# Splitting the second layer's weight loads, and filling 72 rows of each expert's page with the rest by two indirect transfers

## The chip, the cores and the metric

The kernel runs on one core of a Trainium2 chip. A core has TensorE (matmuls), VectorE, ScalarE, GpSimd and SyncE, each with its own instruction stream, and 16 DMA engines that all queues share. SyncE and ScalarE issue plain transfers on queues q1 and q10, GpSimd issues indirect ones on q0. The metric is the device time of one execution in microseconds, median over runs.

## The reference

Four blocks in a row over 64 x 32 tokens of width 256, each of the form `x = x + ffn(cond(x))`. The change touches the end of the first and the second, a mixture of 32 experts of which each token uses 4:

```python
x = x + L0_ffn(L0_cond(x, ...), W1, W2, W3)          # dense feed-forward, hidden width 1024
x = x + L1_ffn(L1_cond(x, ...), gate, gate_up_proj, down_proj)
...                                                   # L2: attention on a paged cache; L3: 8 experts, top 2

def L1_ffn(hidden_states, gate, gate_up_proj, down_proj):   # 32 experts, TOP_K = 4, INTER = 96
    x = hidden_states.reshape(-1, 256)
    routing_weights = softmax(x @ gate)
    top_k_weights, top_k_indices = top_k(routing_weights, 4)   # then normalised to sum 1
    g, u = split(einsum('TD,EDF->TEF', x, gate_up_proj), 2)
    next_states = einsum('TEF,EFD->TED', u * silu(g), down_proj)
    return (next_states * router_weights[..., None]).sum(axis=1)
```

## The kernel before, in words

**First layer (L0), to about 204 us.** Four chunks of 512 tokens (`NCH`), eight hidden pieces each (`M0`). For each piece TensorE makes gate and up (`pe_gate_up`, L447), ScalarE applies silu (L487), VectorE multiplies, and TensorE multiplies down. Between the pieces of chunk c the routing of chunk c-1 for the second layer (called L1 in the code) is done: `pe_rows` (L524), `act_logits` and `act_copies` (L555, L562: each token's row copied four times into `outrows`), VectorE's top-k and slots, `dve_share_half` (L608).

**Scatter into pages.** `sent_d` in DRAM has a region of `SPAN1` = 2176 rows for each of the 32 experts, a row being 260 words (1040 bytes): the token's 256 values, its pair number, its weight. GpSimd scatters each chunk's rows there (`pool_send`, L783, 16 indirect transfers of 128 rows per chunk). `outrows` is used again for each chunk, so `act_copies` of the next chunk waits on `sent` (tiles 0 and 1) or `sent_late` (tiles 2 and 3).

**Fills.** The experts are computed in blocks of 128 rows, so rows after an expert's last token up to the block's end must hold a harmless row (zeros, and a pair number `FAR` that a later bounds check drops). After the last chunk VectorE writes the end row of each expert (`dve_ends`, L653, semaphore `tables`) and then the table of blocks. SyncE (L908 to L910, even experts) and ScalarE (L1192 to L1194, odd ones) each read 16 end rows into a register and issue one fill each: 128 rows from that row on, out of the tile `filler`, of which each partition holds `FILL` = 8 filler rows, so 16 partitions of 8320 bytes (`fill_rows`, L788). One more fill, of the spare page, comes at L905.

**What SyncE's queue does in order, as far as it matters:** segment stores to `newblk` (L870, L872), wait for VectorE's `dest`, three small stores to `dest_d` (L877) and a read-back (L879), a load of `shift` (L881), `tok_d` stores, then gate weights (L890, 3 MB into `big`), wait for the scatters of chunk 1 (`sent_late`), up weights (L892, 3 MB), wait for the end of the first layer, down weights (L899), fills, key load (L914), wait for all 33 fills and all scatters (L916 to L918), then block loads (`sp_block`, L769).

**Expert blocks (L1), from about 262 us.** 95 blocks (`NBK`) in a pipeline: SyncE loads 128 rows, TensorE transposes (L689), makes gate and up (L699), transposes and multiplies down (L717); ScalarE copies and silu (L728, L733), VectorE L745 to L758, GpSimd scatters results to `back_d` (L774). TensorE starts when `big1` says that both weights have landed.

Of the kernel before, what the change touches and what calls it, by code (L numbers as in the profile page):

```python
# [7 lines left out]
ALU = mybir.AluOpType  # L8
# [17 lines left out]
E1, K1, F1 = 32, 4, 96  # L26
E3, K3, F3, FS = 8, 2, 176, 704
# [7 lines left out]
ROW = BLOCK * 2 * G * HD  # L35
# [5 lines left out]
FAR = float(2 ** 17)  # L41
# [24 lines left out]
AT_FILLS, AT_COLS, AT_TABLE = range(1, 4)  # L66
O_CREDIT = 16
FILL = 8
# [5 lines left out]
def constants():  # L74
# [12 lines left out]
    def rows(x):  # L87
# [18 lines left out]
        "ones": np.ones((P, P)),  # L106
    }
# [43 lines left out]
L3 = Experts(E3, K3, 1, F3, ((0, HF3), (HF3, F3)), N3, NB3, NT, NCH + 1, NBK, NBK + NT, AT_TABLE)  # L151
# [18 lines left out]
def build(nc, a):  # L170
    (late_at, _), (first_at, _), (cast_at, _) = constants()
    with ExitStack() as ctx:
# [11 lines left out]
        def at(name, host, word, shape, dt=F32):  # L184

            return nc.alloc_sbuf_tensor_at(name, [P] + shape, dt, offset=base[host] + 4 * word).ap()
# [158 lines left out]
        L1.total = at("total", "rt0", 736, [TPC])  # L345
        L1.onehot = at("onehot", "maskb", 128, [TPC, K1, E1], BF16)
# [324 lines left out]

        def dve_table(dve, L, bank):
            dve.wait_ge(s["table_ps"], 1 if L is L1 else 2)
            nc.vector.tensor_copy(L.table_i[0:2, :], ps[0:2, bank, 0:P]).then_inc(s["tables"], 1)
# [113 lines left out]
        def fill_rows(r, e):  # L788
            p0 = (e * (P // FILL)) % P
            return sent_d[bass.ds(r, P), :].rearrange("(q r) n -> q (r n)", r=FILL), filler[p0:p0 + P // FILL, :]  # L790

# [51 lines left out]
        def _(sp):  # L843
# [29 lines left out]

            sp.wait_ge(s["index"], AT_DESTST)
            for j in range(NEWB):
                src = dest[(j % 2) * B:(j % 2 + 1) * B, (j // 2) * BLOCK:(j // 2 + 1) * BLOCK]
                sp.dma_start(dest_d[:, j * BLOCK:(j + 1) * BLOCK], src).then_inc(s["destld"], 16)  # L877
# [10 lines left out]
            sp.wait_ge(s["segst"], 32)  # L888
            sp.wait_ge(s["index"], AT_TOKST)
            sp.dma_start(l1_gate, a["gate1"]).then_inc(s["big1"], 16)  # L890
            sp.wait_ge(s["sent_late"], 2 * HALF_SENT)
            sp.dma_start(l1_up, a["up1"]).then_inc(s["big1"], 16)  # L892
# [24 lines left out]
            for name in ("sent", "sent_late"):  # L917
                sp.wait_ge(s[name], NCH * HALF_SENT)  # L918
# [40 lines left out]
            sp.wait_ge(s["tables"], AT_TABLE + AT_FILLS)  # L959
# [5 lines left out]
            sp.wait_ge(s["tables"], 2 * AT_TABLE)  # L965
# [24 lines left out]
        def _(pool):  # L990
# [22 lines left out]
            for c in range(NCH):  # L1013
                for h in range(2):
                    tiles, n = slice(2 * h, 2 * h + 2), 2 * c + h + 1
                    if c >= 1:
                        pool.wait_ge(s["sent_late" if h else "sent"], c * HALF_SENT)
                    pool.wait_ge(s["poolhigh"], n)
                    nc.gpsimd.tensor_scalar(outrows[:, tiles, :, D:D + 1].bitcast(I32),
                                            C["pairno"].rearrange("p (t k) -> p t k", t=TPC)[:, tiles, :].unsqueeze(3),  # L1020
                                            float(c * CH * K1), None, ALU.add).then_inc(s["poolhigh"], 1)
                    pool.wait_ge(s["poolhigh"], n + 1)
                    pool.wait_ge(s["numbered"], c + 1 + (h if c == NCH - 1 else 0))
                    pool.wait_ge(s["share_sb"], n)
                    for t in (2 * h, 2 * h + 1):
                        pool.wait_ge(s["rows_sb"], c * TPC + t + 1)
                        pool_send(L1, c, t)

# [321 lines left out]
        def _(dve):  # L1350
# [263 lines left out]
            dve_table(dve, L1, 6)  # L1614
            dve.wait_ge(s["keys"], 16)
# [331 lines left out]
        def _(pe):  # L1947
# [101 lines left out]
            pe.wait_ge(s["big1"], 32)  # L2049
# [409 lines left out]
```

## Time and profile before

| | |
|---|---|
| runs (median of 3, lowest, highest) | 1109.44 us, 1107.39, 1115.31 |
| profiled execution | 1108.0 us, span 1106.2 us |
| TensorE busy | 888.9 us (80%) |
| VectorE, ScalarE, GpSimd busy | 51%, 32%, 32% |
| moved by DMA | 132.3 MB, 120 GB/s on average |

The span is the time from the first to the last instruction of the profiled execution; the time lies 1.8 us above it. Times in rows are microseconds from the span's start. A row of a timeline gives the start, the duration of the group, engine and line, and in brackets how long the engine had been idle and what released it. A row of the busy time by stretch gives the stretch, its length, the busy time of TensorE, TensorE's weight loads, VectorE, ScalarE and GpSimd (with the number of instructions), then TensorE's granted clock, the busy share of the DMA engines and GB/s. TensorE's busy share is an average; what counts for an edit is the stretch that it touches.

### The profile page before, as it was taken

The numbers are of one execution on the slowest core, as the hardware profiler recorded it, in microseconds if no ns is written. First come the engines' busy times: TensorE is split into PE (matmuls) and PEld (weight loads), VectorE is DVE, ScalarE is ACT, GpSimd is POOL, SyncE is SP. The second block draws the span as 40 slices with busy tenths as digits, with TensorE's granted clock in tenths as the row PEclk, the third lists the DMA queues.
The fourth block names the chain that finished last, engine by engine and source line by source line (L and its number), as shares of the span: only waits on it lengthen the run. The fifth ranks groups of instructions, "written<-read, shape, count | busy, mean of one in ns | idle before, by whom it ended". The sixth has DMA issues, their size and how long they took to land.

```text
span 1106.2 us, 17591 instructions
## 1 busy us (share of the span) xinstructions
PE 888.9 (80%) x5301; PEld 684.8 (62%) x5301; DVE 567.5 (51%) x1670; ACT 358.5 (32%) x999; POOL 357.1 (32%) x385
## 2 busy tenths in 40 slices
PE   2999998604889989698147968897986998999976
PEld 2778776403677766574145757787643676777765
DVE  5647885421556645167426757755252434444322
ACT  3434333221333332021135656750252322222210
POOL 7100643550545555123433434200045201444000
PEclk9999999955999999898658888995995998999998
DMA  9151207765634442582257878600142202332231
GB/s 347 15 187 42 78 31 261 227 167 137 186 116 139 123 129 77 185 262 79 79 125 164 176 159 174 165 18 1 38 161 78 94 5 67 104 95 62 75 95 57
DMA packets 68205, 132.26 MB, mean 120 GB/s; under 512 B 19652, under 2 KB 50013, under 8 KB 65123
## 3 DMA queue, kind: packets, MB, share of 16 engines
q1 hardware_dynamic: 47123, 75.81, 23.1%
q0 software_dynamic: 20480, 53.19, 17.8%
q10 hardware_dynamic: 512, 2.13, 0.8%
q8 instruction: 47, 0.77, 0.3%
q14 instruction: 43, 0.35, 0.1%
HBM read 87.39 MB, written 43.30 MB: 118 GB/s over the span
## 4 chain that ended last, share of the span: by engine, by line
PE 30%; DMA 9%; issue 4%; DVE 3%; ACT 2%; SPq 1%; another core or an unknown queue 1%; POOL 1%; DVEq 0%; POOLq 0%; ACTq 0%
PE ps L447 8%; PE ps L699 4%; PE ps L717 3%; DMA early<-early 2%; DMA early<-newblk,new_i 2%; DMA big<-early 2%; DMA early<-in_cache,win_i 2%; PE ps L2329 2%; PE ps L2284 1%; PE ps L2181 1%; PE ps L2223 1%; SPq L945 1%; PE ps L2150 1%; DMA early<-big 1%; PE ps L2285 1%
## 5 line engine op out<-in xcount | busy, mean ns | idle before, releaser
L783 POOL DMA_INDIRECT sent_d<-mid,slot_i x88 | 98.5, 1119 | 122.4 <-DVE mid L608 74.3
L774 POOL DMA_INDIRECT back_d<-early,mid x95 | 93.7, 986 | 107.9 <-DVE early L758 74.2
L717 PE MATMUL ps<-early 96*128 (+1 forms) x346 | 99.3, 388 | 0.1
L745 DVE TENSOR_TENSOR early<-early,ps 128x96 f32<-128x96 f32 (+1 forms) x134 | 37.3, 278 | 119.0 <-ACT early L733 74.7
L728 ACT ACTIVATE early<-ps 128x256 f32<-128x256 f32 x134 | 51.3, 384 | 137.3 <-PE ps L689 130.0
L699 PE MATMUL ps<-big,early 128*128 x380 | 88.3, 356 | 5.8 <-ACT early L728 2.0
L481 DVE TENSOR_TENSOR hidl<-work,hidh 128x512 fp32r<-128x512 f32 (+1 forms) x56 | 38.8, 692 | 97.9 <-ACT hidh L474 96.5
L487 ACT ACTIVATE work<-ps 128x512 f32<-128x512 f32 (+1 forms) x56 | 33.4, 596 | 144.4 <-PE ps L447 138.2
L689 PE MATMUL ps<-late,mid 128*128 128x128 f32 x268 | 52.9, 280 | 33.4 <-DMA mid<-sent_d 33.4
L774 POOL DMA_INDIRECT back_d<-big,mid x39 | 38.4, 984 | 116.9 <-DVE big L758 112.7
L699 PEld LDWEIGHTS ps<-big,early 128*128 128x128 f32 x380 | 61.4, 195 | 19.7 <-issue 16.8
L689 PEld LDWEIGHTS ps<-late,mid 128*128 128x128 f32 x268 | 38.4, 145 | 49.0 <-issue 34.1
L733 ACT ACTIVATE early<-ps 128x96 f32<-128x96 f32 (+1 forms) x134 | 36.2, 270 | 90.8 <-PE ps L699 79.0
L1768 DVE TENSOR_REDUCE early<-ps 128x2 f32<-128x352 f32 x64 | 33.4, 522 | 57.5 <-PE ps L2150 54.6
L717 PEld LDWEIGHTS ps<-early 96*128 96x128 f32 (+1 forms) x346 | 55.4, 191 | 8.8 <-issue 3.5
L447 PE MATMUL ps<-yhigh,l_high 128*128 128x512 f32 x128 | 54.9, 429 | 4.6 <-DVE ylow L1524 3.1
L699 PE MATMUL ps<-early 128*128 x156 | 55.1, 478 | 3.6 <-ACT early L728 3.6
L2150 PE MATMUL ps<-early 128*128 128x176 f32 x256 | 56.8, 351 | 0.0
L1242 ACT ACTIVATE early<-ps,early 128x176 f32<-128x176 f32 x128 | 50.9, 406 | 10.9 <-DVE early L1772 9.7
L474 ACT ACTIVATE hidh<-work 128x512 fp32r<-128x512 f32 (+1 forms) x56 | 35.2, 628 | 52.9 <-DVE work L1545 37.5
L447 PE MATMUL ps<-ylow,l_high 128*128 128x512 f32 x128 | 51.3, 400 | 0.0
L447 PE MATMUL ps<-yhigh,l_low 128*128 128x512 f32 x128 | 51.2, 400 | 0.0
(388 smaller groups left out, 2098.3 us busy)
## 6 DMA issues: line engine op xcount, KB each, us to landing
mid<-sent_d SPq DMA_DIRECT2D x134, 130.0 KB
big<-back_d SPq DMA_DIRECT2D x16, 512.0 KB
early<-back_d SPq DMA_DIRECT2D x16, 256.0 KB, 3.4
early<-in_w SPq DMA_DIRECT2D x3, 1024.0 KB, 12.3
big<-in_gate SPq DMA_DIRECT2D x1, 3072.0 KB, 12.4
big<-in_up SPq DMA_DIRECT2D x1, 3072.0 KB, 11.0
early<-in_gu SPq DMA_DIRECT2D x1, 2816.0 KB, 10.5
big<-big SPq DMA_DIRECT2D x24, 96.0 KB
```

The source lines that it names most:

```text
L447: last = nc.tensor.matmul(out, w, x, start=start and n == 0, stop=stop and n == 2)
L481: nc.vector.tensor_tensor(low[0:w, slot, :], silu[0:w, slot, :], high[slot][0:w, :], ALU.subtract).then_inc(s["hid_ready"], 1)
L689: last = nc.tensor.transpose(ps[:, b % 2, k * P:(k + 1) * P], xblk[b % XRING][:, k * P:(k + 1) * P], ident)
L699: last = nc.tensor.matmul(ps[:, 2 + j % 2, 0:2 * F].rearrange("p (g n) -> p g n", g=2), L.yTb[j % 2][:, k * P:(k + 1) * P], L.gu[:, :, k, ...
L717: last = nc.tensor.matmul(ps[:, 6 + j % 2, 0:D], L.hTb[j % 2][0:f1 - f0, h * P:(h + 1) * P], L.down[0:f1 - f0, h, bass.ds(owners[j] * D, D ...
L728: nc.scalar.activation(L.yTb[b % 2], ps[:, b % 2, 0:2 * P], ACT.Copy).then_inc(s["turn_sb"], 1)
L733: nc.scalar.activation(L.sgb[(b - 1) % 2], ps[:, 2 + (b - 1) % 2, 0:L.F], ACT.Silu)\
L745: nc.vector.tensor_tensor(L.hb[j % 2], L.sgb[j % 2], ps[:, 2 + j % 2, F:2 * F], ALU.mult)\
L774: nc.gpsimd.indirect_dma_start(out=back_d, out_offset=bass.IndirectOffsetOnAxis(ap=xblk[b % XRING][:, D:D + 1].bitcast(I32), axis=0), in_= ...
L783: nc.gpsimd.indirect_dma_start(out=sent_d, out_offset=bass.IndirectOffsetOnAxis(ap=L.slot_i[:, i:i + 1], axis=0), in_=L.rows[c][:, t, n, : ...
L1242: last = nc.scalar.activation(Pex[:, n % 2, h, :], ps[:, 2 + n % 2, h * WK:(h + 1) * WK], ACT.Exp, bias=acol[:, 1, n % 2, h:h + 1], scale= ...
L2150: last = nc.tensor.matmul(ps[:, 2 + n % 2, h * WK:(h + 1) * WK], Qbd[:, (n // 2) % 2, n % 2, h * P:(h + 1) * P], KTs[:, n % 2, :], start=F ...
```

## The change

Three things change together.

1. The gate and up weights of the second layer are loaded in five pieces instead of two, each piece as soon as the part of `big` under it is free: of 6144 words per partition each, 4096 of gate after the segment stores, 3072 of up before the `dest_d` stores, and the other three pieces after the wait for `sent_late`. TensorE waits for 80 instead of 32.
2. A fill writes 72 rows instead of 128, as 18 partitions of 4 rows (4160 bytes each).
3. The rows from there to the block's end are written in aligned pieces of 8 rows. VectorE computes, for each of 32 x 8 possible pieces, its index, or one out of bounds where the piece lies behind the block's end (`dve_rest`). GpSimd writes them by two indirect transfers of up to 128 pieces of 8320 bytes each, after all fills have landed; SyncE waits for them on `sent`.

```diff
-FILL = 8
+FILL, FILLED, RUN = 8, 72, 4
...
+        def dve_rest(dve, ch):
+
+            piece, invalid, page_end = (L1.tabf[:, 0:E1], L1.ends[:, 0, :], L1.ends[:, 2, :])
+            ch.link(nc.vector.tensor_scalar(piece, L1.running, 1.0 / FILL, FILLED / FILL - 0.5 + 0.5 / FILL, ALU.mult,
+                                            ALU.add))
+            ch.link(nc.vector.tensor_scalar(piece, piece, MAGIC, None, ALU.add))
+            ch.link(nc.vector.tensor_scalar(piece, piece, MAGIC, None, ALU.subtract))
+            ch.link(nc.vector.scalar_tensor_tensor(page_end, L1.ends[:, 1, :], float(P), C["region"][:, 0:E1], ALU.mult,
+                                                   ALU.add))
+            ch.link(nc.vector.tensor_scalar(piece, piece, C["piece"], None, ALU.add))
+            ch.link(nc.vector.scalar_tensor_tensor(invalid, piece, float(FILL), page_end, ALU.mult, ALU.is_ge))
+            ch.link(nc.vector.scalar_tensor_tensor(piece, invalid, FAR, piece, ALU.mult, ALU.add))
...
+            ch.link(nc.vector.tensor_reduce(rest_f, by16, X, ALU.add))
+            nc.vector.tensor_copy(rest_i, rest_f).then_inc(s["tables"], 1)
...
         def fill_rows(r, e):
-            p0 = (e * (P // FILL)) % P
-            return sent_d[bass.ds(r, P), :].rearrange("(q r) n -> q (r n)", r=FILL), filler[p0:p0 + P // FILL, :]
+            n = FILLED // RUN
+            p0 = n * (e % (P // n))
+            return (sent_d[bass.ds(r, FILLED), :].rearrange("(q r) n -> q (r n)", r=RUN),
+                    filler[p0:p0 + n, 0:RUN * ROWW])
...
+            gate, up = a["gate1"].rearrange("p k n -> p (k n)"), a["up1"].rearrange("p k n -> p (k n)")
+            G1, U0, U1 = ROW, ROW + 4496 - KD * N1, ROW + 7568 - KD * N1
+            sp.wait_ge(s["segst"], 32)
+            sp.dma_start(big[:, 0:G1], gate[:, 0:G1]).then_inc(s["big1"], 16)
             sp.wait_ge(s["index"], AT_DESTST)
+            sp.dma_start(big[:, KD * N1 + U0:KD * N1 + U1], up[:, U0:U1]).then_inc(s["big1"], 16)
             for j in range(NEWB):
...
-            sp.wait_ge(s["segst"], 32)
             sp.wait_ge(s["index"], AT_TOKST)
-            sp.dma_start(l1_gate, a["gate1"]).then_inc(s["big1"], 16)
             sp.wait_ge(s["sent_late"], 2 * HALF_SENT)
-            sp.dma_start(l1_up, a["up1"]).then_inc(s["big1"], 16)
+            sp.dma_start(big[:, G1:KD * N1], gate[:, G1:KD * N1]).then_inc(s["big1"], 16)
+            for u0, u1 in ((0, U0), (U1, KD * N1)):
+                sp.dma_start(big[:, KD * N1 + u0:KD * N1 + u1], up[:, u0:u1]).then_inc(s["big1"], 16)
...
-            for name in ("sent", "sent_late"):
-                sp.wait_ge(s[name], NCH * HALF_SENT)
+            sp.wait_ge(s["sent_late"], NCH * HALF_SENT)
+            sp.wait_ge(s["sent"], NCH * HALF_SENT + 16 * E1 * FILL // P)
...
+            pool.wait_ge(s["tables"], AT_REST)
+            pool.wait_ge(s["filled"], 16 * (E1 + 1))
+            for j in range(E1 * FILL // P):
+                nc.gpsimd.indirect_dma_start(
+                    out=sent_d.rearrange("(q r) n -> q (r n)", r=FILL),
+                    out_offset=bass.IndirectOffsetOnAxis(ap=rest_i[:, j:j + 1], axis=0), in_=filler, in_offset=None,
+                    bounds_check=(SPARE1 + P) // FILL - 1, oob_is_err=False).then_inc(s["sent"], 16)
...
             dve_table(dve, L1, 6)
+            dve_rest(dve, ch)
...
-            pe.wait_ge(s["big1"], 32)
+            pe.wait_ge(s["big1"], 80)
```

Left out are two constants (17 columns of `late`), two small tiles, and the counts that `tables` has to reach in the second expert layer (L3 in the code), whose own fills (L961 to L964, 128 rows from 128 partitions) stay as they are.

## Rows read from the trace of the kernel before

**Rows 1.** Waits (us in total, times, longest), 200-265 us, TensorE and SyncE.
```profile
PE ps L689 <- DMA mid<-sent_d: 32.3, 1, 32.3
SPq L918 <- DMA sent_d<-work: 1.8, 1, 1.8
```

**Rows 2.** Busy time by stretch; last columns: TensorE's clock, DMA share, GB/s.
```profile
230.00:249.00 19.00, 0.59 (x2) 0.09 (x2) 1.88 (x11) 0.00 (x0) 12.70 (x14) 0.50 0.85 212
249.00:262.00 13.00, 0.00 (x0) 0.00 (x0) 0.00 (x0) 0.00 (x0) 0.00 (x0) 0.50 0.82 176
```

**Rows 3.** Timeline (start, duration, engine, line), SyncE and ScalarE, 229-287 us.
```profile
230.06 29.32 SPq L910 DMA_DIRECT2D sent_d<-work  x16
259.43 0.42 SPq L914 DMA_DIRECT2D zm<-in_first  x1
262.52 24.69 SPq L769 DMA_DIRECT2D mid<-sent_d  x17
229.72 27.25 ACTq L1194 DMA_DIRECT2D sent_d<-work  x16
```

**Rows 4.** Timeline, VectorE and GpSimd, 224 to 246 us.
```profile
224.84 0.17 DVE L608 TENSOR_TENSOR mid<-share,total 128x8 f32<-128x8 f32 x1
228.60 0.20 DVE L653 CAST endrow_i<-running 128x32 int32<-128x32 f32 x1
225.89 1.03 POOL L783 DMA_INDIRECT sent_d<-mid,slot_i  x1 [5.58 <-DVE mid L608]
245.43 0.96 POOL L783 DMA_INDIRECT sent_d<-mid,slot_i  x1 [0.30 <-issue]
```

**Rows 5.** Transfers (packets, MB, share of engines), GpSimd's queue, 248-249 us.
```profile
q0 software_dynamic: 14, 0.03, 7.7%
```

**Rows 6.** Timeline, ScalarE, two chunks of the first layer.
```profile
136.14 0.60 ACT L487 ACTIVATE work<-ps 128x512 f32<-128x512 f32 x1 [1.67 <-PE ps L447]
151.94 0.60 ACT L487 ACTIVATE work<-ps 128x512 f32<-128x512 f32 x1 [1.91 <-PE ps L447]
180.88 0.60 ACT L487 ACTIVATE work<-ps 128x512 f32<-128x512 f32 x1 [1.65 <-PE ps L447]
187.63 1.03 ACT L562 ACTIVATE mid<-ps 128x1024 f32<-128x1024 f32 x1 [3.73 <-DMA sent_d<-mid,slot_i]
198.88 0.60 ACT L487 ACTIVATE work<-ps 128x512 f32<-128x512 f32 x1 [1.47 <-PE ps L447]
```

**Rows 7.** Who waited for whom, 179 to 200 us, TensorE.
```profile
PE ps L536 <- DVE chosen L627: 2.2, 1, 2.2
```

**Rows 8.** Timeline, SyncE and GpSimd, 136 to 190 us.
```profile
136.92 1.73 SPq L877 DMA_DIRECT2D dest_d<-big  x3
165.85 0.34 SPq L881 DMA_DIRECT2D big<-in_first  x1
176.44 1.15 SPq L890 DMA_DIRECT2D big<-in_gate  x1
178.24 0.96 POOL L783 DMA_INDIRECT sent_d<-mid,slot_i  x1 [0.30 <-issue]
```

**Rows 9.** Busy time by stretch, first layer, 91 to 108 us.
```profile
91.00:108.00 17.00, 17.00 (x81) 13.71 (x80) 11.24 (x33) 8.85 (x14) 0.00 (x0) 1.00 0.01 1
```

**Rows 10.** Transfers by queue, 226-262 us: SyncE's (q1), ScalarE's (q10).
```profile
q1 hardware_dynamic: 656, 2.31, 35.7%
q10 hardware_dynamic: 512, 2.13, 24.0%
```

**Rows 11.** Timeline, SyncE, the later expert layer's fills.
```profile
867.29 8.42 SPq L964 DMA_DIRECT2D sent_d<-big  x8
```

**Rows 12.** DMA issues of the page (KB each, median us to landing).
```profile
big<-in_gate SPq DMA_DIRECT2D x1, 3072.0 KB, 12.4
big<-in_cache,seg_i POOLq DMA_INDIRECT x2, 8.5
```

**Rows 13.** Transfers, 797 to 815 us, where L954 and L958 run.
```profile
DMA packets 2275, 4.34 MB, mean 241 GB/s; under 512 B 354, under 2 KB 1762, under 8 KB 2274
```

More of the change, by code:

```diff
@@ L65 @@
 AT_CONDX, AT_TABST, AT_CONDIDX, AT_ROWPS, AT_DESTST, AT_SHIFT, AT_TOKST, AT_FOLDS = range(1, 9)
-AT_FILLS, AT_COLS, AT_TABLE = range(1, 4)
+AT_FILLS, AT_COLS, AT_TABLE, AT_REST = range(1, 5)
 O_CREDIT = 16
-FILL = 8
+FILL, FILLED, RUN = 8, 72, 4
 MAGIC = 1.5 * 2 ** 23
@@ L106, in constants @@
         "ones": np.ones((P, P)),
+        "piece": p[:, None] % FILL,
+        "pieceof": (p[:, None] // FILL) == np.arange(P // FILL)[None, :],
     }
@@ L150 @@
 L1 = Experts(E1, K1, 0, F1, ((0, F1),), N1, NBK, 0, 0, 0, 0, 0)
-L3 = Experts(E3, K3, 1, F3, ((0, HF3), (HF3, F3)), N3, NB3, NT, NCH + 1, NBK, NBK + NT, AT_TABLE)
+L3 = Experts(E3, K3, 1, F3, ((0, HF3), (HF3, F3)), N3, NB3, NT, NCH + 1, NBK, NBK + NT, AT_REST)
 L1.pieces = [(c, 0, TPC) for c in range(NCH - 1)] + [(NCH - 1, 0, 2), (NCH - 1, 2, TPC)]
@@ L345, in build @@
         L1.total = at("total", "rt0", 736, [TPC])
+        rest_f = at("rest_f", "rt0", 744, [E1 * FILL // P])
+        rest_i = at("rest_i", "rt0", 752, [E1 * FILL // P], I32)
         L1.onehot = at("onehot", "maskb", 128, [TPC, K1, E1], BF16)
@@ L670, in dve_ends @@
             nc.vector.tensor_scalar(cols2[:, 1:2], owner, float(E - 1), None, ALU.min).then_inc(s["tables"], 1)
+        def dve_rest(dve, ch):
[9 more added lines that the diff above has]
+            ch.link(nc.vector.scalar_tensor_tensor(piece, invalid, FAR, piece, ALU.mult, ALU.add))
+            by16 = piece.rearrange("p (j k) -> p j k", k=P // FILL)
+            ch.link(nc.vector.tensor_tensor(by16, by16,
+                                            C["pieceof"].unsqueeze(1).broadcast_to([P, E1 * FILL // P, P // FILL]),
+                                            ALU.mult))
+            ch.link(nc.vector.tensor_reduce(rest_f, by16, X, ALU.add))
+            nc.vector.tensor_copy(rest_i, rest_f).then_inc(s["tables"], 1)
         def dve_table(dve, L, bank):
@@ L958, in _ @@
                         sp.dma_start(L3.down[r0:r1, h, e * D:(e + 1) * D], a["down3"][p0:p0 + r1 - r0, m, :])                            .then_inc(s["down3"], 16)
-            sp.wait_ge(s["tables"], AT_TABLE + AT_FILLS)
+            sp.wait_ge(s["tables"], AT_REST + AT_FILLS)
             sp.wait_ge(s["fill_set"], 3)
@@ L964, in _ @@
                 sp.dma_start(sent_d[bass.ds(r, P), :], filler3).then_inc(s["filled"], 16)
-            sp.wait_ge(s["tables"], 2 * AT_TABLE)
+            sp.wait_ge(s["tables"], AT_REST + AT_TABLE)
             sp.wait_ge(s["filled"], 16 * (E1 + 1 + E3 + 1))
```

## The prediction

> **What bounds the kernel now.** I read the waits first, then the engines in the stretch that the longest wait names, then the transfers in it.
>
> The waits of TensorE between 200 and 265 us hold one that dwarfs the rest: 32.3 us in which its first transpose of the second layer's expert blocks (L689) waits for rows loaded from `sent_d` [rows 1]. The windows show what the core does meanwhile. From 230 to 249 us TensorE, VectorE and ScalarE are as good as idle while the DMA engines are busy 0.85 of the time at 212 GB/s; from 249 to 262 us no engine computes at all, and the DMA engines are busy 0.82 at 176 GB/s [rows 2]. So whatever shortens this stretch shortens the kernel, microsecond for microsecond, as long as its end is set by the same chain. What sets that end is the queues' work in order: VectorE gives the end rows of the 32 pages at 228.60, SyncE issues 16 fills from 230.06 for 29.32 us, ScalarE the other 16 from 229.72 for 27.25 us. SyncE then issues the key load at 259.43, waits 1.8 us for the last fill, and sends for the first block at 262.52 [rows 3, 4]. I put the landing of the last fill at 259.43 + 0.42 + 1.8 = 261.7. GpSimd's 16 scatters of the last token chunk run in the same stretch, issued from 225.89 to 246.4 [rows 4]. They are not last: from 248 to 249 us their queue moves 14 packets, 0.03 MB, its last of the stretch [rows 5]. The fills are last, by some 13 us.
>
> A second, small bound lies in the first layer. Its last token chunk goes slower than the one before. From the silu (L487) at 136.14 to the one at 151.94 four steps took 15.80 us; the same four from 180.88 to 198.88 took 18.00 us. Between them stands an idle time of 3.73 us in which ScalarE's copy (L562, at 187.63) waits for the scatters into `sent_d`, and TensorE waits 2.2 us for what follows from it [rows 6, 7]. The scatter it waits for was issued at 178.24, and the gate weights' 3 MB had been issued at 176.44 [rows 8]. A load of 3 MB and the scatters' packets shared the DMA engines, and the scatters came in 9 us after their issue. The last scatters of the next stretch took under 3.6 us (the last one issued at 245.43, landed by 249) [rows 4, 5].
>
> **The change, part by part.**
>
> *The weights.* 2.1 MB of gate go at the end of the segment stores (about 92 us), 1.6 MB of up ahead of the `dest_d` stores (136.92), and the rest, 2.6 MB, behind the wait for `sent_late`. At 91 to 108 us the DMA engines are busy 0.01 [rows 9]. What is moved past on SyncE's queue are the three small `dest_d` stores of 136.92, their read-back and the `shift` load; these would come about 5 us later, and between the stores at 136.92 and the issue of `shift` at 165.85 SyncE has only the read-back to do [rows 8]. So I cost it at nothing; the cover is over 20 us thick, and with it gone every late microsecond of the `dest_d` rows would hold VectorE's `token_rows`. What the weights give is not their own landing, since TensorE wants them only at 262. It is that no load is in flight beside the scatters that end with the one of 178.24. These then land by 178.24 + 3.6 = 181.8, before ScalarE asks (at 183.9, 3.73 us before its copy), and the wait goes. TensorE's chunk is then the one of 15.80 us: **-2.2 us**, which passes on to the residual, the routing and the fills. Bounds: 0, if another wait takes its place, and 3.7.
>
> *The fills.* Each fill shrinks from 128 rows of 1040 bytes to 72, so the 32 fills move 2.4 MB where they moved 4.26 MB (2.13 MB on each of the queues q1, with one spare page and the key load more, and q10) [rows 10]. Nothing in the number of issues changes. Two limits remain. The floor is the issue itself: one register load and one issue. The fills of the later expert layer (L964), eight in 8.42 us with the last taking 0.33, come every (8.42 - 0.33) / 7 = 1.16 us, and they are alone [rows 11]. The present pace is 29.32 / 16 = 1.83 us on average. The ceiling on pace while GpSimd scatters is the traffic. A scatter of 133 KB every 1.27 us (16 in 20.5 us) [rows 4] is 105 GB/s out of 212, which leaves 107 GB/s for a pair of fills, one from each queue. Such a pair is 150 KB now instead of 266, so 1.40 us instead of 2.5. Until the scatters are gone (by 249) that makes 13 pairs; the other three go at the floor. Last issue: 230.06 + 12 x 1.40 + 3 x 1.16 = 250.3; landed 1.5 later (as the 1.8 now, with less in it), 251.8. Against 261.7 that is **-9.9 us**. Bounds: all at the floor, last issue 247.5, landed 249.0, -12.7; and no gain at all, if something other than the bytes sets the pace (rivals).
>
> *The rest.* GpSimd now waits for all 33 fills and then issues two indirect transfers, for whose landing SyncE waits before the first block. This is new and lies wholly on the path. From VectorE's share (L608, ended 225.01) to GpSimd's first scatter at 225.89 it took 0.9; the second issue follows 1.3 after the first; the last scatter landed 2.6 to 3.6 after its start, of which I take 3.0 [rows 4, 5]. Sum: **+5.2 us**. The nearest row above it is the gather of 128 rows of 16 KB, 8.5 us to landing [rows 12], which would make 10.7. It moved 2.1 MB, though. Of the 2 x 128 pieces of 8.3 KB only those between row 72 after the end and the page's end are written; with ends spread evenly over a page, 56 of 128 experts need some and 28 rows on average, 12 rows per expert and about 0.4 MB in all, plus rounding. So I stay with the lower row. Bounds +4.8 and +10.7.
>
> *The ten VectorE operations* of `dve_rest` are about 0.2 us each and end before 236, while the fills run for another 15 us: nothing. What waits behind them on VectorE is the key load, which comes after the fills. Seventeen more columns of `late`: nothing. ScalarE issues its 16 fills as before. Behind GpSimd's new wait stand only the scatters of the blocks' results, which need the blocks first, so it delays nothing of its own.
>
> Sum on the profiled execution: 1108.0 - 2.2 - 9.9 + 5.2 = 1101.1. The median shown is 1.4 us above that execution, so the same sum on the median is **1102.5 us**, 0.6% less.
>
> **Rivals.**
>
> *Nine engines.* A fill used to be 16 rows of 8320 bytes, which 16 engines can share evenly. Now it is 18 rows of 4160 bytes. If a transfer only uses as many engines as divide its rows, that is nine with two rows each, 8320 bytes per engine, exactly what an engine carried before. The trace has a place to look: 26 loads of 8 to 88 rows together with one of 128 partitions leave 354 packets under 512 bytes [rows 13]. If each engine used leaves one completion packet, the 26 leave 338, which is 13 per load and not 16. The row counts follow from the code (88, 40, 48, 80, 8, ...), and the largest divisor up to 16 of each adds up to 338 exactly. So nine engines it very likely is. What I doubt is that this sets the pace: an engine's fills and scatters together are 4.26 + 2.13 MB over 16, 400 KB in 32 us or 12 GB/s, where the gate load's 3.1 MB in 12.4 us [rows 12] make 16 GB/s per engine, with scatters beside it. If it does set it all the same, the fills land at 261.7 as now and the new tail is simply added: 1109.4 - 2.2 + 5.2 = **1112.5**. This is the case on the other side. It decides as soon as the fills come in less than 3.0 us earlier than now.
> The Trainium skill, page "DMA: Bandwidth & Descriptors", section "Why a DMA increments its semaphore by 16 and not by 1", states the divisor rule itself: a transfer from SyncE or ScalarE is split over the largest number up to 16 that divides the slowest dimension of both sides. The 338 packets agree with it, and by it the fills run on nine engines.
>
> *The scatters, not the bytes, slow the issue.* Then the fills go on at one in (249 - 230) / 8 = 2.4 us, if half of them fall there, until the scatters are gone and at the floor after it: 8 done at 249, eight more at 1.16, landed at 259.8. Gain 1.9, tail 5.2, weights 2.2: +1.1, **1110.5**. For it: the pace. SyncE's 16 issues took 29.32 us [rows 3]; eight at 2.4 and eight at 1.3 make just that. Against: even without scatters 1.3 is above the floor of 1.16, with 176 GB/s moving [rows 2].
>
> *Everything at the floor.* Fills land at 249.0: -2.2 - 12.7 + 5.2 = -9.7, **1099.7**. For it: the steadier row of the later expert layer. Against: no scatters run beside that one.
>
> *The weights do nothing* and the wait at 187.63 has another source: 2.2 us more on each of the above.
>
> *A dear tail* of 10.7 adds 5.5 to any of them.
>
> **How the numbers follow.** The forecast has 0.50, nine engines 0.22, the scatters 0.10, the floor 0.13, and 0.05 for a dear tail or what I have not seen. The time is that of the likeliest, 1102.5, with its own range of 1099 to 1106. The whole range reaches from below the floor case to above nine engines: **1098 to 1114**. Within 1% (11.1 us, about what a measurement of this kernel can tell from no change) lie all the cases named at their own prices; over it on the fast side is only the floor with a stall less (0.12), on the slow side only nine engines with a dear tail (0.04).
>
> **What would show it.** Of the changed kernel: the copy at L562 of the last chunk no longer waits for `sent_d`, and four silu steps take 15.8. The 16 issues on each queue take about 20 us instead of 29 and 27. GpSimd's two transfers of fillers start about 252, and the first block's load about 5.5 us after. If the queues still take 27 us or more, the bytes were not the limit; if the first two transfers take over 8 us, the tail was mis-sized; if TensorE's wait for the first block is unchanged or longer, gain and tail have cancelled.

## The result, and the profile after

| | before | after |
|---|---|---|
| runs beside each other on one chip, median | 1110.08 us | 1115.94 us |
| lowest to highest | 1106.07 to 1115.31 | 1111.64 to 1121.46 |
| profiled span | 1106.2 us | 1114.1 us |

The changed kernel is slower: ratio 1.0066, 95% interval 1.0036 to 1.0096, so 4 to 11 us. That is still within 1%, but 13 us above the predicted time, beyond the upper end of the range, and of the other sign than the forecast.

The same stretch as in [rows 3, 4], start and duration of each group, SyncE, ScalarE and GpSimd of the changed kernel:

```profile
226.70 30.16 ACTq L1232 DMA_DIRECT2D sent_d<-work  x16
226.99 30.54 SPq L940 DMA_DIRECT2D sent_d<-work  x16
242.43 0.96 POOL L806 DMA_INDIRECT sent_d<-mid,slot_i  x1 [0.30 <-issue]
257.57 0.38 SPq L944 DMA_DIRECT2D zm<-in_first  x1
259.86 0.99 POOL L1062 DMA_INDIRECT sent_d<-work,rest_i  x1 [16.48 <-DMA sent_d<-work]
261.16 0.99 POOL L1062 DMA_INDIRECT sent_d<-work,rest_i  x1 [0.30 <-issue]
...
266.58 7.38 SPq L792 DMA_DIRECT2D mid<-sent_d  x7
```

The 16 fills take 30.54 us on SyncE where they took 29.32, although each moves little more than half the bytes. The busy time by stretch (as in [rows 2]: DMA share and GB/s last) says what did not hold them up:

```profile
230.00:249.00 19.00, 0.00 (x0) 0.00 (x0) 1.90 (x9) 0.00 (x0) 10.29 (x12) 0.50 0.47 145
249.00:258.00 9.00, 0.00 (x0) 0.00 (x0) 0.00 (x0) 0.00 (x0) 0.00 (x0) 0.50 0.38 103
```

The DMA engines fell from 0.85 and 0.82 busy to 0.47 and 0.38, and the issues did not speed up. And TensorE's wait for the first block, 32.3 us in [rows 1], grew (waits, 200 to 285 us):

```profile
PE ps L712 <- DMA mid<-sent_d: 39.6, 2, 39.3
POOL sent_d L1062 <- DMA sent_d<-work: 16.5, 1, 16.5
```

From the start: SyncE's first fill is issued 3.1 us earlier than before (226.99 against 230.06), the 16 issues cost 1.2 us more, and from the key load to the first block's load it takes 9.01 us instead of 3.09, so 5.9 more. 266.58 is 4.1 us later than 262.52. Another 3.8 us up to the end came behind this place; a second trace of the same kernel, below, doesn't have them.

### The profile page after: what moved, and what is told of

Its sections match the earlier page's. It is cut to its first block, busy times and chain, and to the rows that moved or that the text cites. A ratio compares the mean times of both kernels' runs of the same rounds, so it can differ in the third digit from the quotient of the medians.

```text
span 1114.1 us, 17609 instructions
## 1 busy us (share of the span) xinstructions
PE 886.1 (80%) x5301; PEld 682.8 (61%) x5301; DVE 570.3 (51%) x1680; ACT 357.9 (32%) x999; POOL 358.7 (32%) x387
## 4 chain that ended last, share of the span: by engine, by line
PE 27%; DMA 10%; issue 5%; DVE 3%; ACT 2%; SPq 1%; another core or an unknown queue 1%; POOL 1%; DVEq 0%; POOLq 0%; ACTq 0%
PE ps L451 8%; PE ps L722 4%; PE ps L740 3%; DMA big<-in_cache,win_i 2%; DMA big<-newblk,new_i 2%; DMA early<-in_cache,win_i 2%; PE ps L2368 2%; DMA early<-newblk,new_i 2%; PE ps L2220 1%; PE ps L2323 1%; PE ps L2262 1%; DMA early<-early 1%; DMA early<-big 1%; SPq L975 1%
## 5 line engine op out<-in xcount | busy, mean ns | idle before, releaser
L2189 PE MATMUL ps<-early 128*128 128x176 f32 x256 | 54.5, 340 | 0.0
L781 DVE TENSOR_SCALAR early<-ps,mid 128x256 f32<-128x256 f32 x95 | 45.1, 475 | 14.0 <-PE ps L740 11.9
L732 PE MATMUL ps<-late,early 128*96 128x128 f32 (+1 forms) x173 | 41.9, 279 | 11.7 <-DVE early L768 11.5
```

Source lines behind the costliest of these rows:

```text
L732: last = nc.tensor.transpose(ps[0:f1 - f0, 4 + j % 2, h * P:(h + 1) * P], L.hb[j % 2][:, f0:f1], ident)
L781: nc.vector.tensor_scalar(L.ob[j % ORING], ps[:, 6 + j % 2, 0:D], xblk[j % XRING][:, D + 1:D + 2], None, ALU.mult).then_inc(s["out_sb"], 1)
L2189: last = nc.tensor.matmul(ps[:, 2 + n % 2, h * WK:(h + 1) * WK], Qbd[:, (n // 2) % 2, n % 2, h * P:(h + 1) * P], KTs[:, n % 2, :], start=F ...
```

## The experiments

Three theories stood against each other after the trace above. **A:** while GpSimd issues its scatters, every instruction of SyncE's and ScalarE's sequencers is slow, and a fill is six of them (load of the end row into a register, two register operations, an assertion, a move, the issue), so neither bytes nor engines matter. **C:** nine engines set the pace. **D:** bytes or packets do after all. The view that separates them is how fast the queues issue while the scatters run (to about 245 us) and behind them.

**The weights alone** (`e1_weights`): the kernel before with these edits.

```diff
...
+            sp.wait_ge(s["segst"], 32)
+            sp.dma_start(big[:, 0:G1], gate[:, 0:G1]).then_inc(s["big1"], 16)
             sp.wait_ge(s["index"], AT_DESTST)
+            sp.dma_start(big[:, KD * N1 + U0:KD * N1 + U1], up[:, U0:U1]).then_inc(s["big1"], 16)
...
-            sp.dma_start(l1_gate, a["gate1"]).then_inc(s["big1"], 16)
             sp.wait_ge(s["sent_late"], 2 * HALF_SENT)
-            sp.dma_start(l1_up, a["up1"]).then_inc(s["big1"], 16)
+            sp.dma_start(big[:, G1:KD * N1], gate[:, G1:KD * N1]).then_inc(s["big1"], 16)
+            for u0, u1 in ((0, U0), (U1, KD * N1)): ...
```

> The kernel before with the weight loads alone split as in the changed kernel; fills of 128 rows, no rest. Theory A (the weights' part of the change is sound, the loss is all in fills and tail): the wait of the row copies for the scatters goes, four silu steps of the last chunk take 15.7 us instead of 18.0, the end rows come 1.7 to 3 us earlier, and the first block's load about 2 us before 262.5, total 1108 us (-2). Rival B (what the weights give is lost again in the expert blocks, since the changed kernel's blocks fell back by some 4 us between 262 and 453 us): the same first block load, but the blocks end no earlier than before, total 1110 us or more.

Measured: ratio 0.9985 (0.9956 to 1.0013), 1107.6 against 1109.4 us. The wait is gone, SyncE's first fill starts at 227.47 and the first block's load at 258.63. From VectorE's first result of a block to its last it took 171.8 us, where the two traces of before have 172.1 and 169.0, so nothing is lost in the blocks and B finds no support. (They end 4.9 us before those of the first trace of before, but only about half a us before those of the second.) The time agrees with A's 2 us, but can't tell it from nothing.

**Sixteen engines** (`e2_fills64`), the changed kernel with one number altered:

```diff
-FILL, FILLED, RUN = 8, 72, 4
+FILL, FILLED, RUN = 8, 64, 4
```

> The changed kernel with fills of 64 rows (16 partitions of 4160 bytes, so 16 engines of equal load) instead of 72 rows (18 partitions, nine engines); the rest starts one piece of 8 rows earlier. Theory A (while GpSimd scatters, each instruction of SyncE's and ScalarE's sequencers is slow, whatever the fill moves): SyncE's 16 issues still take 30 us (29 to 31.5), first block load at 266 to 267, total as the changed kernel, 1116 us. Rival C (nine engines set the pace): the packets spread over 16 engines, 16 issues in 20 us or less, first block load about 256, total 1106 us.

**A ninth of the rows** (`e3_fills8`): fills of 8 rows, now 8 partitions of one row (1040 bytes) each, and four indirect transfers for the rest:

```diff
-FILL, FILLED, RUN = 8, 72, 4
+FILL, FILLED, RUN = 8, 8, 4
...
-            n = FILLED // RUN
-            p0 = n * (e % (P // n))
-            return (sent_d[bass.ds(r, FILLED), :].rearrange("(q r) n -> q (r n)", r=RUN),
-                    filler[p0:p0 + n, 0:RUN * ROWW])
+            p0 = FILLED * (e % (P // FILLED))
+            return sent_d[bass.ds(r, FILLED), :], filler[p0:p0 + FILLED, 0:ROWW]
...
-            for j in range(E1 * FILL // P):
+            for j in range(2 * E1 * FILL // P):
                 nc.gpsimd.indirect_dma_start(
```

> The changed kernel with fills of only 8 rows (8.3 KB, a ninth of the bytes); four indirect transfers of up to 128 pieces write the rest. Theory A: the pace doesn't depend on the bytes; SyncE's 16 issues take 28 to 30 us while scatters run at 2.6 us a pair, and only the tail grows: four issues instead of two (+2.6 us) and about 2.1 MB instead of 0.6 (+5 to +8 us), first block load about 275, total 1124 us. Rival D (the bytes or the packets of the fills hold the issue after all, in queue or engines): the 16 issues take under 22 us, and the first block load comes at 266 or earlier, total 1115 us or less.

SyncE's timeline of the 64-row kernel, then of the 8-row one:

```profile
228.43 27.57 SPq L940 DMA_DIRECT2D sent_d<-work  x16
256.04 0.42 SPq L944 DMA_DIRECT2D zm<-in_first  x1
265.02 9.23 SPq L792 DMA_DIRECT2D mid<-sent_d  x8
```

```profile
227.95 29.83 SPq L940 DMA_DIRECT2D sent_d<-work  x16
257.82 0.38 SPq L944 DMA_DIRECT2D zm<-in_first  x1
271.26 3.70 SPq L794 DMA_DIRECT2D mid<-sent_d  x4
```

The 8-row kernel settles D. Its fills move 8 KB each, the DMA engines are nearly idle once the scatters are gone (stretches as above), and 16 issues still take 29.83 us:

```profile
230.00:245.00 15.00, 0.48 (x2) 0.00 (x0) 3.42 (x17) 0.00 (x0) 10.95 (x13) 0.50 0.31 108
247.00:258.00 11.00, 0.00 (x0) 0.00 (x0) 0.00 (x0) 0.00 (x0) 0.00 (x0) 0.50 0.06 12
```

Where the time is, the instructions of the two lines of a fill on SyncE show (count, then shortest, median and longest in ns, then first and last start). First while scatters run, 230 to 245 us:

```profile
L939 SPq TENSOR_LOAD <-endrow_i x5: 6/502/699, 229.5 to 243.0; - x5
L939 SPq SEQ_ASSERT  x5: 3/700/708, 230.9 to 243.8; - x5
L940 SPq FUSED_REGOPS  x5: 6/699/708, 230.9 to 244.5; - x5
L940 SPq DMA_DIRECT2D sent_d<-work x4: 13/696/709, 232.3 to 241.6; - x4
```

and behind them, 247 to 258 us:

```profile
L939 SPq TENSOR_LOAD <-endrow_i x8: 482/484/567, 247.4 to 256.5; - x8
L939 SPq SEQ_ASSERT  x8: 18/18/18, 248.1 to 257.3; - x8
L940 SPq DMA_DIRECT2D sent_d<-work x9: 316/316/317, 247.0 to 257.5; - x9
L940 SPq FUSED_REGOPS  x8: 37/37/37, 248.1 to 257.3; - x8
```

```profile
L939 SPq SEQ_ASSERT  x5: 7/11/207, 230.7 to 242.8; - x5
L940 SPq MOVE sent_d<-work x4: 3/479/700, 231.4 to 240.6; - x4
```

The start times of the records show the pattern. Beside the scatters SyncE gets on in steps of 0.70 us, with one to three instructions in a step, and a fill takes three to six steps. A fill costs (241.6 - 232.3) / 3 = 3.1 us in the 8-row kernel's first stretch and (257.5 - 247.0) / 8 = 1.31 in its second.

Full DMA engines alone don't do this. In the kernel before, behind the scatters, they are 0.82 busy at 176 GB/s ([rows 2]), and SyncE's small instructions are as quick there as anywhere, 249 to 262 us:

```profile
L909 SPq SEQ_ASSERT  x8: 18/18/18, 249.8 to 258.9; - x8
L910 SPq FUSED_REGOPS  x8: 37/37/37, 249.9 to 258.9; - x8
```

The 64-row kernel shows that C is not nothing either. SyncE's issues of line 940 after 245 us, changed kernel first, then 64 rows:

```profile
L940 SPq DMA_DIRECT2D sent_d<-work x10: 317/318/698, 244.9 to 257.2; - x10
```

```profile
L940 SPq DMA_DIRECT2D sent_d<-work x9: 314/314/315, 247.1 to 255.7; - x9
```

and ScalarE's, in the same order:

```profile
L1232 ACTq DMA_DIRECT2D sent_d<-work x7: 516/517/532, 247.4 to 256.3; - x7
```

```profile
L1232 ACTq DMA_DIRECT2D sent_d<-work x8: 2/322/322, 247.0 to 254.3; - x8
```

On sixteen engines a fill takes 1.08 us behind the scatters (8.6 / 8) and ScalarE's issue 322 ns; on nine it takes 1.37 (12.3 / 9) and 517. SyncE's own issue is no dearer, 318 ns against 314. What takes longer there is the load of the end row into a register, 247 to 264 us, changed kernel first, then 64 rows:

```profile
L939 SPq TENSOR_LOAD <-endrow_i x8: 489/536/804, 246.2 to 256.0; - x8
```

```profile
L939 SPq TENSOR_LOAD <-endrow_i x8: 266/270/274, 247.5 to 255.0; - x8
```

The 128-row fills of the kernel before, on sixteen engines, had 524 ns as the median of that load, and the 8-row fills 484, so the number of engines is not the only thing that lengthens it.

The packets of the changed kernel's fills are the count that nine engines leave: in 226 to 258.6 us ScalarE's queue moved

```profile
q10 hardware_dynamic: 432, 1.20, 13.1%
```

432 packets for 16 fills, 27 each: 18 of data and nine completions. The Trainium skill, page "DMA: Bandwidth & Descriptors", section "Why a DMA increments its semaphore by 16 and not by 1", gives the divisor rule, and the trace agrees.

The 27.57 us for 16 fills are neither A's 29 to 31.5 nor C's 20. Beside the scatters 64 rows are no faster than 128, but slower (the next section has a table); behind them the number of engines counts. The times: 64 rows 1.0003 (0.9970 to 1.0036), 1111.2 us, where A had 1116; 8 rows 1.0046 (1.0015 to 1.0077), 1116.4 us, where A had 1124. The first block's load came at 271.26 instead of the expected 275, since the bytes of four transfers took less time than I gave them.

**Fills behind the scatters** (`e5_late`): the 64-row kernel with two waits before the fills on both queues, and nothing else.

```diff
+            sp.wait_ge(s["sent"], NCH * HALF_SENT)
+            sp.wait_ge(s["sent_late"], NCH * HALF_SENT)
             for e in range(0, E1, 2):
```

> As the changed kernel with 64-row fills, but SyncE and ScalarE wait with their fills until all of GpSimd's scatters have landed (near 246 us). Theory A (only the scatters make the queues' instructions slow): the same 16 issues on each queue now come every 1.07 us from the first on, 16 to 17.5 us in all instead of 27.6; last issue near 263, first block load near 272, total 1118 us. Rival G (two queues at once, or the row registers, are slow by themselves): 22 us or more.

```profile
246.85 16.82 ACTq L1236 DMA_DIRECT2D sent_d<-work  x16
246.94 16.99 SPq L942 DMA_DIRECT2D sent_d<-work  x16
```

A gave 16 to 17.5 us; it is 16.99 instead of 27.57, with both queues working and the same registers. The fills started 18.5 us later and ended 7.9 us later, and the first block's load came at 273.01 (A: near 272). G falls. The time of the single run was 1113.98 us, 4 below what A said.

**Issues without registers** (`e6_static`):

```diff
             for e in range(0, E1, 2):
-                r = sp.value_load(L1.endrow_i[0:1, e:e + 1], min_val=e * SPAN1, max_val=e * SPAN1 + T)
-                sp.dma_start(*fill_rows(r, e)).then_inc(s["filled"], 16)
+                sp.dma_start(*fill_rows(e * SPAN1 + T, e)).then_inc(s["filled"], 16)
```

> All of the pages' fillers are written by six indirect transfers of GpSimd's; SyncE and ScalarE issue 16 fills each of 64 rows at the same time, but at fixed rows that nobody reads (row 2048 of each region), so without a register load: of the six instructions of a fill only the issue itself is left. Theory A (each sequencer instruction pays about 0.7 us while GpSimd issues indirect transfers, so the count of instructions sets the pace): 16 issues in 8 to 20 us, 0.5 to 1.3 us each, instead of 2.9 while scatters run. Rival H (the issue of a transfer alone is what is held up): the pace stays at 2.2 us or more while scatters run. The total says little; near 1110 us.

```profile
L948 SPq DMA_DIRECT2D sent_d<-work x16: 348/563/1256, 226.1 to 236.6; - x16
```

Sixteen issues in 10.5 us while scatters run, 0.70 each: with one instruction per fill instead of six the pace is about four times as high. H falls. The issue itself is slowed too, 563 ns instead of 314, but here the DMA engines are 0.87 busy at 237 GB/s, so the bytes may have a part in that. (This kernel's time, 1112.47 us in its single run, is no measure: its plain fills write rows that nobody reads.)

**Fewer plain fills** (`e4_hybrid`). If GpSimd goes on at its 1.27 us per transfer while the others crawl, it should have part of the fills. Experts 16 to 31 get no plain fill; VectorE computes for each the single rows up to the next multiple of 8 and the aligned pieces from there to the page's end. These touch nothing that another transfer writes, so GpSimd doesn't wait for `filled`:

```diff
+            ch.link(nc.vector.tensor_scalar(c8[:, G], L1.running[:, G], 1.0 / FILL, 0.5 - 0.5 / FILL, ALU.mult,
+                                            ALU.add))
...
-            for e in range(0, E1, 2):
+            for e in range(0, EH, 2):
...
-            pool.wait_ge(s["filled"], 16 * (E1 + 1))
+            pool.wait_ge(s["fill_set"], 2)
+            for j in range(2):
+                nc.gpsimd.indirect_dma_start(
+                    out=sent_d.rearrange("(q r) n -> q (r n)", r=FILL), ...
+            nc.gpsimd.indirect_dma_start(
+                out=sent_d, out_offset=bass.IndirectOffsetOnAxis(ap=rest_i[:, 2:3], axis=0),
+                in_=filler[:, 0:ROWW], ...
```

> The split weights, and the fills divided: experts 0 to 15 by 16 plain fills of 128 rows (8 on SyncE, 8 on ScalarE), experts 16 to 31 by three indirect transfers behind GpSimd's scatters (rows up to the next multiple of 8 by single rows, then aligned pieces of 8 rows up to the page's end), which overlap nothing and so wait for no fill. Theory A (a pair of plain fills costs 2.6 us while GpSimd scatters, whatever is in it, and GpSimd's own pace of 1.27 us is undisturbed): 8 pairs end at 227 + 8 x 2.6 = 248, GpSimd's three at 242.4 + 3 x 1.3 = 246.3, landed at 251, first block load at about 252 (262.5 before), total 1100 us. Rival E (the added transfers of about 1 MB share a full path with the fills): landed at 258 or later, total 1106 us or more.

> The divided fills (16 plain, three indirect transfers) once more, beside the changed kernel on the same chip. If the gain is real: ratio 0.992 again, 0.989 to 0.996, and 12 to 15 us under the changed kernel; its first profile had the end rows 3.6 us later than with the split weights alone, by chance or because of its 17 VectorE operations behind them; they come after the end rows, so by chance, and here the first block load should be at 253 to 256 instead of 257.3.

Its second trace, ScalarE, SyncE and the last two of GpSimd's three:

```profile
227.85 20.48 ACTq L1240 DMA_DIRECT2D sent_d<-work  x8
228.19 23.37 SPq L944 DMA_DIRECT2D sent_d<-work  x8
246.22 1.00 POOL L1066 DMA_INDIRECT sent_d<-work,rest_i  x1 [0.30 <-issue]
247.52 0.99 POOL L1070 DMA_INDIRECT sent_d<-work,rest_i  x1 [0.30 <-issue]
251.60 0.42 SPq L948 DMA_DIRECT2D zm<-in_first  x1
255.80 24.53 SPq L798 DMA_DIRECT2D mid<-sent_d  x17
```

Ratio 0.9922 (0.9887 to 0.9957) and again 0.9922 (0.9885 to 0.9958), 1102.3 and 1102.7 us: 8.7 us faster than before by the ratio, 7.2 and 7.8 by the medians, and the second 13.5 below the median of the changed kernel beside it. The first block's load, 257.27 and 255.80, lies 5.2 us in mean before that of the two traces of before; the rest of the 8.7 is not shown by the traces, but the interval, 4.7 to 12.8 us, holds 5.2 too. The load came 5 us later than the 252 expected first, and at the upper end of the 253 to 256 expected then, because eight fills of SyncE took 23.2 and 23.4 us, not 20.8. In the second trace a register operation of SyncE still takes 0.71 us at 250.42, when GpSimd's last scatter of tokens has been issued for over 6 us and only its further transfers are still in flight: they hold up the last fills in the same way.

**Where to divide** (`e7_hybrid8`: experts 0 to 7 by plain fills; `e8_all`: none).

```diff
-FILL, EH = 8, 16
+FILL, EH = 8, 8
...
```

With `EH` the indirect transfers change: eight experts share one of aligned pieces and sixteen one of single rows, so these kernels have five and six of them instead of three.

> Split weights; experts 0 to 7 by 8 plain fills (4 on each queue), experts 8 to 31 by five indirect transfers (three of aligned pieces, two of single rows) behind GpSimd's scatters. Theory A: 4 pairs of plain fills end at 227.5 + 4 x 2.9 = 239, so GpSimd is the last: 244.2 + 5 x 1.3 = 250.7, landed 253.5, first block load 254.5 where the split weights alone had 258.6; total 1102 to 1104 us, level with the division at 16. Rival E (the added bytes, about 1.6 MB by pieces, land late): first block load at 258 or later, total 1107 us or more.

> Split weights; no plain fills at all but the spare page, all 32 experts' fillers by six indirect transfers behind the scatters. Theory A: GpSimd's last issue at 244.2 + 6 x 1.3 = 252, about 2.1 MB to land in 3 to 6 us, first block load at 256 to 259, total 1104 to 1108 us. Rival E (the pieces' bytes set the end): first block load at 262 or later, total 1111 us or more.

0.9949 (0.9911 to 0.9987), 1105.8 us, and 0.9944 (0.9912 to 0.9977), 1105.1 us; first block loads at 256.56, 2 us behind what A said, and 257.70, where A had it. Both beat the kernel before; among the three divisions the runs can't choose. With no plain fills GpSimd's last transfer started at 250.80 and the block's load came 6.9 us later. A page of the Trainium skill, "Perfetto Trace Analysis", section "DMA Optimizations", advises to balance transfers over SyncE, ScalarE and GpSimd where their issue is the bottleneck; these runs agree, with the addition that here the queues are not independent.

**Once more, and the rest of the change alone** (`e9_again`, the changed kernel unaltered; `e10_fills_only`, without the weights' edits; `e12_before`).

> The changed kernel once more, unaltered. Theory I (its profiled execution lost 4.6 us in the expert blocks, from +4.2 at the first block to +8.7 at the end of the blocks, by chance): this execution's blocks take as long as before's (first result of a block to the last 172.1 us, plus or minus 2), and the clock at 168 to 170 us may be at either level; the queues again take 30 us for 16 fills. Rival J (the change slows the blocks): 175 us or more again. Total 1114 to 1117 us.

> The kernel before with the fills of 72 rows and the rest alone; the weights' loads stay as they were. If the parts add up: the end rows as before (228.6), 16 fills on SyncE in 30.5 us (+1.1), key load to first block load 9.0 us (+5.9), first block load at 269.5 (+7), total 1116 to 1118 us, ratio 1.006. Rival K (the split weight loads make the fills dearer): ratio 1.002 or less.

> The kernel before, unaltered, for a second trace. To see how far two executions of one kernel lie apart at the end rows, the first block load (262.5), the blocks (172.1 us) and the clock at 168 to 170 us (1.00 in the first trace): within 3 us each.

SyncE of `e9_again`, then of `e10_fills_only`:

```profile
228.41 31.10 SPq L940 DMA_DIRECT2D sent_d<-work  x16
259.56 0.38 SPq L944 DMA_DIRECT2D zm<-in_first  x1
268.59 11.07 SPq L792 DMA_DIRECT2D mid<-sent_d  x9
```

```profile
229.12 31.05 SPq L935 DMA_DIRECT2D sent_d<-work  x16
260.21 0.38 SPq L939 DMA_DIRECT2D zm<-in_first  x1
269.25 9.32 SPq L792 DMA_DIRECT2D mid<-sent_d  x8
```

Ratios 1.0064 (1.0033 to 1.0095) and 1.0101 (1.0059 to 1.0143). The first repeats the result. Its blocks took 172.9 us from the first result to the last, where the changed kernel's first execution had 176.0 and before's two 172.1 and 169.0: I, not J. The second is dearer than the 1.006 expected, which its interval still holds, and K falls. Its fills and its tail are as expected, but in its trace a part that no edit touches, the attention's scores (64 matmuls of L2147 in the kernel before, from about 560 us on), took 174.8 us, against 165.7 and 169.6 in the two traces of before and 163 to 174 in the others. That is one execution; why all six runs lie so high isn't shown. So one profile, or the total of one execution, says nothing of a few us in this kernel; the stretch from the first fill to the first block does.

## Why the prediction was wrong, step by step

From SyncE's first fill to the first block's load, all us, with the parts:

| kernel | first fill to first block | 16 fills | key load to block |
|---|---|---|---|
| before, two traces | 32.46, 31.51 | 29.32, 28.45 | 3.09, 3.01 |
| split weights alone | 31.16 | 28.05 | 3.06 |
| changed, two traces | 39.59, 40.18 | 30.54, 31.10 | 9.01, 9.03 |
| 72-row fills and rest alone | 40.13 | 31.05 | 9.04 |
| 64-row fills | 36.59 | 27.57 | 8.98 |
| 64-row fills behind the scatters | 26.07 | 16.99 | 9.03 |
| 8-row fills | 43.31 | 29.83 | 13.44 |
| divided, two traces | 26.27, 27.61 | (8) 23.18, 23.37 | 3.05, 4.20 |

*The fills, predicted -9.9, came to +2.3* (30.9, the mean of the three kernels with 72 rows, against 28.6). This is the step that failed, and with it the forecast: "The ceiling on pace while GpSimd scatters is the traffic". I saw DMA engines 0.85 busy beside slow issues and divided the GB/s by the bytes of a fill. The traffic was what the issues made, not what held them. The 8-row fills show it: no faster at a ninth of the bytes. What holds them is that a fill is six sequencer instructions, which get on in steps of 0.70 us while the scatters are in flight. The trace of before couldn't tell the two: the traffic gave 2.5 us for a pair of fills beside the scatters, the rival 2.4, and SyncE's second to seventh fill came every 2.7 us there. "One register load and one issue", the prediction's floor, was wrong too.

The rival "the scatters, not the bytes, slow the issue" was the mechanism. It had 0.10, because its 1.3 us behind the scatters lay above the floor of 1.16 and 176 GB/s were moving then. That objection was true for 128 rows (the 64-row fills come at 1.08 in that stretch) but says nothing of the stretch before it. Its time, 1110.5, was still 5 us low, mostly since it gave the fills a gain of 1.9 us, and they lost 2.3.

Where they lost shows when the 16 are divided at SyncE's seventh, the last beside the scatters or the one just behind them. Of the kernel before, the last ten issues (the changed kernel's stand above, 244.9 to 257.2):

```profile
L910 SPq DMA_DIRECT2D sent_d<-work x10: 3/315/700, 245.2 to 259.1; - x10
```

| rows in a fill | first to seventh fill | seventh to last |
|---|---|---|
| 128, three traces | 15.1, 13.8, 13.7 | 13.9, 14.4, 14.1 |
| 72, three traces | 17.9, 18.7, 18.6 | 12.3, 12.1, 12.1 |
| 64 | 16.5 | 10.8 |
| 8 | 18.6 | 10.9 |

Behind the scatters the 72-row fills did gain, 1.9 us in mean. Beside them they lost 4.2. No theory had that; A has the pace unchanged. Why smaller fills are slower there stays open.

*Nine engines* had a rival's time, 1112.5, with the fills landing when they did before. The engines are nine, and against sixteen they cost 3.3 us (30.9 against 27.6, one trace), though not by the bytes per engine that I worked out: 1.4 us of it lie behind the scatters, where a fill takes 1.37 us against 1.08, and 1.9 beside them, unexplained. With sixteen engines the smaller fills would have been worth 1.0 us. The times agree in direction, 1.0003 against 1.0066, but their intervals are too wide to tell 3.3 us from twice that.

*The tail, predicted +5.2, was +6.0* (9.03 against 3.05). GpSimd's first transfer started 2.3 us after the key load's issue, the second 1.30 later as said, and the block's load 5.4 us after that. The sum is near by luck, in part. The landing that I took as 3.0 took at most those 5.4, nearly halfway to the gather's 8.5. In return GpSimd's first transfer didn't come 0.9 us behind the moment when the block's load would have gone (3.05 after the key load), but 0.8 ahead of it.

*The weights, predicted -2.2.* The mechanism was right: the copy's wait for the scatters is gone in all traces with split weights. ScalarE's silus of the changed kernel, the two that answer to 136.14 and 198.88 in [rows 6]:

```profile
134.78 0.60 ACT L491 ACTIVATE work<-ps 128x512 f32<-128x512 f32 x1 [1.66 <-PE ps L451]
196.84 0.60 ACT L491 ACTIVATE work<-ps 128x512 f32<-128x512 f32 x1 [1.83 <-PE ps L451]
```

The four steps of the last chunk took 15.68 us, as predicted. But between these two lie 62.06 us against 62.74: only 0.7 was kept. TensorE's granted clock tells where the rest went. 168 to 170 us, before, then changed (columns as in [rows 2], the clock third from last):

```profile
168.00:170.00 2.00, 2.00 (x8) 1.31 (x7) 1.30 (x3) 0.64 (x1) 1.70 (x2) 1.00 0.92 361
```

```profile
168.00:170.00 2.00, 2.00 (x4) 0.88 (x3) 1.73 (x2) 0.09 (x1) 1.65 (x2) 0.50 0.57 220
```

TensorE stood for some 3.4 us in both, until 167.67 and 166.29, waiting for VectorE. In the trace of before the clock stayed at 2.4 GHz afterwards, in the changed kernel's it was at 1.2 GHz, and one step took 8.48 instead of 6.83 us. That is no effect of the change: in the second trace of before it fell too (0.60). Of all fourteen traces, twelve have 0.50 to 0.60 in these 2 us, one 0.78, and the first of before alone 1.00. And where it falls, the chunk is later and waits less. Waits for `sent_d` in that second trace and in the kernel with fills alone, for the 3.7 of [rows 6]:

```profile
ACT mid L562 <- DMA sent_d<-mid,slot_i: 2.4, 1, 2.4
```

```profile
ACT mid L566 <- DMA sent_d<-mid,slot_i: 1.2, 1, 1.2
```

So the term was read off one execution in which the stall was at its largest. The same stretch is 62.7 to 63.1 us in the three traces without split weights and 62.0 to 62.1 in ten of the eleven with them; the eleventh, of the first divided kernel, has 63.0. That is 0.9 us without the exception, 0.8 with it. The end rows of these eleven came 1.3 us earlier in mean than those of the three (226.8 against 228.1), so more than the last chunks may have gained. By the traces the term was mis-sized by a factor of about two; the time of the split weights alone, between 4.9 us less and 1.4 more, can't tell 0.9 from 2.2.

*The sum* with the measured terms: -0.9 + 2.3 + 6.0 = +7.4 us. The ratio 1.0066 of 1110 makes 7.3. *The ten VectorE operations* cost nothing, as predicted.

The upper end of the range, 1114, was the nine-engine case with 1.5 us on top, and that case had the fills land as late as before, no later. "No gain at all" was the lower bound of the term; that the fills could get slower, I gave no room. Nor does the sentence on 1% come out: nine engines with a dear tail make 1112.5 + 5.5 = 1118.0, outside the stated range but within 1% of 1109.4.

## What stays open

Why a sequencer's instruction takes 0.70 us beside GpSimd's indirect transfers was not tried. The runs show that it is so on both queues, that any of the six instructions can be the one, that it ends when the scatters have landed, and that fills of a ninth of the bytes don't escape it. Two readings remain that they don't separate: that GpSimd's issuing does it, or that its packets in flight do. The second is favoured, though not shown, by the end: the last slow step of the 64-row kernel ends at 247.0, 3.2 us after its last scatter was issued, and in the kernel with the late fills the scatters had landed 3.4 us after the last one's issue. Open is also why smaller fills are slower than 128 rows beside the scatters, and why a fill of 18 or 8 partitions takes ScalarE 517 ns to issue and one of 16 partitions of 4160 bytes 322, while SyncE's stays at 314 to 318 and its register load is longer instead.

## What to carry to other kernels

A busy DMA share beside slow issues doesn't make the bytes the limit, and a model that gives the old pace isn't confirmed by it when its rival gives it too: look at the issuing queue's own instructions first, and ask what each of them, the register operations too, takes in that stretch against a quiet one. If it is the issues, fewer bytes per issue are worth next to nothing; fewer instructions, fewer issues, or the engine whose pace is undisturbed, are worth the whole. And a transfer that must wait for the end of a chain costs its full latency, here 6 us, so make it disjoint instead of late.

## What the runs showed of the hardware that was not expected

- While GpSimd issued a scatter every 1.27 us, SyncE's second to seventh fill, six instructions each, came every 2.5 to 2.7 us with 128 rows and every 3.1 to 3.4 with 72, 64 or 8, in steps of 0.70; with no scatters and both queues at work, 64 rows took 1.1. GpSimd's pace stayed at 1.27 in all kernels.
- Issues without register instructions went at 0.70 us beside the same scatters.
- A transfer of 18 or 8 partitions took ScalarE 517 ns to issue, one of 16 partitions of 4160 bytes 322.
- The load of a register from SBUF took 264 to 291 ns in 15 loads of the 64-row fills behind the scatters (median 272), and 484 as the median of the 8-row fills there. The Trainium skill, page "DMA: Bandwidth & Descriptors", section "Latency and other measured facts", gives a floor of about 600 ns for it; the trace doesn't agree.
- TensorE's clock after a stall of 3.4 us was 2.4 GHz in one execution of a kernel and 1.3 to 1.4 in mean in another of the same kernel; the step that followed took 6.83 us and 8.52.
